# A state-space layer's recurrence: four PSUM banks for the broadcasts of delta, two for those of delta times x, and the convolution's taps over two steps

## The reference, cut to what matters

```python
u = up_x @ W_up + b_up
left, right = jnp.split(u, 2, axis=-1)
xp = jnp.pad(left, ((0, 0), (K - 1, 0), (0, 0)))
conv = sum((conv_w[:, k] * xp[:, k:k + Lq, :] for k in range(K))) + conv_b      # K = 3
x = jax.nn.silu(conv)
delta = jax.nn.softplus(x @ W_delta + b_delta)
Bm = x @ W_B + b_B
Cm = x @ W_C + b_C
dA = jnp.exp(delta[..., None] * A)
dBx = delta[..., None] * Bm[:, :, None, :] * x[..., None]
# over the tokens:  h = dA_t * h + dBx_t ;  y_t = einsum('bdn,bn->bd', h, C_t)
gated = (y + D_skip * x) * jax.nn.silu(right)
return gated @ W_down + b_down
```

## Time and profile before

| | |
|---|---|
| device time, median of 3 runs | 1930.89 us (1929.56 to 1931.49) |
| the profiled execution | 1928.22 us, of which the span of the profile is 1926.4 us |
| PE busy over the span | 1773.1 us (92%) |
| DVE busy | 1467.3 us (76%) |
| ACT busy | 902.1 us (47%) |
| POOL busy | 752.5 us (39%) |
| the loop of this layer | from 1269 to 1732 us of the span |

### The profile page before, as it was taken

The page is one execution under the profiler, slowest core; times in us unless marked ns, Lnnn a source line. Parts: engine busy times, 40 slices in busy tenths (PEclk is TensorE's granted clock), DMA queues, the critical chain, the costliest instruction groups (busy, mean ns, idle before and its releaser), DMA issues. The chain is left out here.

```text
span 1926.4 us, 23846 instructions
## 1 busy us (share of the span) xinstructions
PE 1773.1 (92%) x7613; PEld 938.9 (49%) x7613; DVE 1467.3 (76%) x2421; ACT 902.1 (47%) x2115; POOL 752.5 (39%) x850
## 2 busy tenths in 40 slices
PE   6879999999999799989998999988898988889999
PEld 2346654555555466646665555533332333335555
DVE  5868865655555488857777788789999999988886
ACT  3335544555546355435565333455465554333332
POOL 4832222334333223332210000068989899770000
PEclk9989999999999899979999999999999999899999
DMA  6000000000000000010000000000000000000000
GB/s 257 1 1 1 1 0 1 1 1 1 1 1 1 1 1 1 1 44 1 2 2 1 1 1 1 1 17 6 12 1 17 1 11 6 1 1 1 1 6 17
DMA packets 9787, 20.20 MB, mean 10 GB/s; under 512 B 1088, under 2 KB 8384, under 8 KB 8768
## 3 DMA queue, kind: packets, MB, share of 16 engines
q1 hardware_dynamic: 9664, 18.68, 2.8%
HBM read 14.48 MB, written 1.05 MB: 8 GB/s over the span
## 5 line engine op out<-in xcount | busy, mean ns | idle before, releaser
L2103 POOL TENSOR_TENSOR ssm_hc<-ssm_h,ssm_cm 128x512 f32<-128x512 f32 x256 | 324.5, 1288 | 47.3 <-DVE ssm_h L2157 46.1
L307 PE MATMUL banks<-ffn_x_high,up_high 128*128 128x512 f32 x544 | 282.2, 519 | 10.2 <-ACT ffn_s1g L857 6.2
L2042 PE MATMUL banks<-ssm_hc,const 128*128 128x512 f32 x512 | 269.1, 608 | 0.2
L2157 DVE TENSOR_TENSOR_SCAN ssm_h<-banks,ssm_dbx 128x512 f32<-128x512 f32 x208 | 248.0, 1207 | 5.3 <-issue 3.3
L2087 ACT ACTIVATE banks<-banks,a_neg 128x510 f32<-128x510 f32 x256 | 167.1, 659 | 171.4 <-PE banks L2018 170.0
L309 PE MATMUL banks<-ffn_x_high,up_low 128*128 128x512 f32 x544 | 216.1, 397 | 0.0
L308 PE MATMUL banks<-ffn_x_low,up_high 128*128 128x512 f32 x544 | 215.9, 397 | 0.0
L1504 POOL TENSOR_SCALAR wide_pin<-wide_pin,wide_rden 128x256 f32<-128x256 f32 x256 | 117.6, 478 | 223.0 <-DVE wide_rden L1522 223.0
L343 POOL TENSOR_TENSOR x_norm<-x_centred,x_square 128x512 f32<-128x512 f32 x32 | 41.5, 1297 | 392.9 <-ACT x_square L338 392.9
L1739 ACT ACTIVATE ffn_th<-banks 128x512 f32<-128x512 f32 (+1 forms) x136 | 81.2, 597 | 213.7 <-PE banks L309 191.6
L307 PEld LDWEIGHTS banks<-ffn_x_high,up_high 128*128 128x128 f32 x544 | 102.7, 189 | 98.8 <-issue 43.9
(11 more groups left out here) (228 smaller groups left out, 3518.1 us busy)
## 6 DMA issues: line engine op xcount, KB each, us to landing
ssm_packed<-ssm_parts SPq DMA_DIRECT2D x48, 64.0 KB, 2.0
up_whole<-in_up SPq DMA_DIRECT2D x1, 2304.0 KB, 14.9
weights<-in_weights SPq DMA_DIRECT2D x1, 2048.0 KB, 23.2
up_whole<-in_up SPq DMA_DIRECT2D x1, 2048.0 KB, 7.9
half<-in_half SPq DMA_DIRECT2D x1, 1440.0 KB, 17.9
weights<-in_weights SPq DMA_DIRECT2D x1, 1168.0 KB, 25.4
weights<-in_weights SPq DMA_DIRECT2D x1, 1152.0 KB, 7.9
const<-in_const SPq DMA_DIRECT2D x1, 1042.0 KB, 9.9
```

The source lines that it names most:

```text
L307: pe.matmul(out, w_high, x_high, start=True, stop=False)
L2042: pe.matmul(k.bank[5][:], k.c("hot")[:, P - row:2 * P - row], hc[:, i % LAG, :], start=False, stop=(i % NP == NP - 1)).then_inc(s["red"], 1)
L2103: pool.tensor_tensor(hc[:, i % LAG, :], h[:, i % HOLD, :], cm[:, i // NP % 2, :], ALU.mult) \
L2157: dve.tensor_tensor_scan(h[:, n % HOLD, :], k.bank[DELTA[n % AHEAD]][:], product, 0.0, ALU.mult, ALU.add).then_inc(s["h"], 1)
```

## The change

Four things are changed together.

1. `DELTA` gets a fourth bank (bank 6), and `DELTA_X` keeps two (2 and 3). PE, in turn i, now does `spread_delta(i + 1)` and then `spread_dx(i + 1)`. `spread_delta(i + 1)` waits for the scan of step i - 3, `spread_dx(i + 1)` for the product or the copy of step i - 1.
2. ACT's copy for a pooled step k is made in turn k, after the exponential of step k, where it was made in turn k - 1 before the exponential of step k - 1. The place of POOL's product among POOL's instructions stays what it was (it is written at the head of a turn where it was written at the end of the turn before).
3. The convolution: two taps at step 22, the third at step 23.
4. Every piece behind it is one step later: SiLU at 24, delta at 31, and so on to the last cut at 58.

```diff
-    AHEAD, HOLD, LAG = 3, 4, 6
-    DELTA, DELTA_X = (0, 1, 4), (2, 3, 6)
+    AHEAD, BEHIND, HOLD, LAG = 4, 2, 4, 6
+    DELTA, DELTA_X = (0, 1, 4, 6), (2, 3)
...
+    def convolve(pe, tap):
+        return pe.matmul(two(k.bank[7]), w(f"conv{tap}"), left[:, :, tap:L + tap], start=(tap == 0), stop=(tap == 2))
...
         if n == 22:
             pe.wait_ge(s["right_in"], p + 1)
             pe.wait_ge(s["cleared"], 1)
-            for tap in range(3):
-                ins = pe.matmul(two(k.bank[7]), w(f"conv{tap}"), left[:, :, tap:L + tap],
-                                start=(tap == 0), stop=(tap == 2))
-            ins.then_inc(s["conv"], 1)
-        if n == 30:
+            for tap in range(2):
+                convolve(pe, tap)
+        if n == 23:
+            convolve(pe, 2).then_inc(s["conv"], 1)
+        if n == 31:
...
-        if n == 23:
+        if n == 24:
             act.wait_ge(s["conv"], p + 1)
...
-        if n in (50, 51, 56, 57):
-            part, v = (n - 44) // 6, (n - 44) % 6
+        if n in (51, 52, 57, 58):
+            part, v = (n - 45) // 6, (n - 45) % 6
             act.wait_ge(s["rest"], 4 * p + 2 * (part - 1) + v + 1)
...
-        if n in (46, 47, 52, 53):
-            part, v = (n - 46) // 6, (n - 46) % 6
+        if n in (47, 48, 53, 54):
+            part, v = (n - 47) // 6, (n - 47) % 6
...
-                if i >= AHEAD and by_pool(i - AHEAD):
-                    pe.wait_ge(s["dx_in"], pooled[i - AHEAD + 1])
-                elif i >= AHEAD:
-                    pe.wait_ge(s["dbx"], i - AHEAD + 1 - pooled[i - AHEAD + 1])
-                pe.matmul(k.bank[DELTA_X[i % AHEAD]][:], k.h("pick")[0:96, c * P:(c + 1) * P],
+                if i >= BEHIND and by_pool(i - BEHIND):
+                    pe.wait_ge(s["dx_in"], pooled[i - BEHIND + 1])
+                elif i >= BEHIND:
+                    pe.wait_ge(s["dbx"], i - BEHIND + 1 - pooled[i - BEHIND + 1])
+                pe.matmul(k.bank[DELTA_X[i % BEHIND]][:], k.h("pick")[0:96, c * P:(c + 1) * P],
...
             pe.wait_ge(s["resets"], 1)
+            spread_delta(0)
             spread_dx(0)
             for i in range(ALL + LAG):
                 if i + 1 < ALL:
+                    spread_delta(i + 1)
                     spread_dx(i + 1)
-                if i < ALL:
-                    spread_delta(i)
...
             for i in range(ALL):
-                if i + 1 < ALL and by_pool(i + 1):
-                    m = pooled[i + 1]
-                    act.wait_ge(s["bx"], i + 2)
-                    if m >= 2:
-                        act.wait_ge(s["pdbx"], m - 1)
-                    act.activation(dxs[:, m % 2, :], k.bank[DELTA_X[(i + 1) % AHEAD]][:], ACT.Copy).then_inc(s["dx_in"], 1)
                 act.wait_ge(s["bc"], i + 1)
                 spot_i = two(k.bank[DELTA[i % AHEAD]])[:, :, 1:]
                 act.activation(spot_i, spot_i, ACT.Exp, scale=k.a_neg[:, i % NP:i % NP + 1]).then_inc(s["da"], 1)
+                if by_pool(i):
+                    m = pooled[i]
+                    act.wait_ge(s["bx"], i + 1)
+                    if m >= 2:
+                        act.wait_ge(s["pdbx"], m - 1)
+                    act.activation(dxs[:, m % 2, :], k.bank[DELTA_X[i % BEHIND]][:], ACT.Copy).then_inc(s["dx_in"], 1)
...
-    return Stage(s, home, NP, {"ffn1": (10, 14, 15, 20, 22, 23, 26, 29, 32, 35, 39, 42, 44, 48, 52, 54, NP)},
+    return Stage(s, home, NP, {"ffn1": (10, 14, 15, 20, 22, 23, 27, 30, 33, 36, 40, 43, 45, 49, 53, 55, NP)},
```

More of the change, by code:

```diff
@@ L1926, in scalar @@
                 k.table(act, "natural_log_exp_and_others")
-        if n == 31:
+        if n == 32:
             act.wait_ge(s["delta"], p + 1)
             act.activation(z[:], k.bank[7][:], ACT.Identity, bias=w("b_delta")).then_inc(s["z"], 1)
-        if n == 32:
+        if n == 33:
             act.wait_ge(s["z"], p + 1)
@@ L1934, in scalar @@
             act.activation(e[:], e[:], ACT.Exp, scale=-1.0).then_inc(s["e"], 1)
-        if n == 33:
+        if n == 34:
             act.wait_ge(s["e"], p + 1)
             act.activation(u[:], e[:], ACT.Identity, bias=1.0).then_inc(s["u"], 1)
-        if n == 34:
+        if n == 35:
             act.wait_ge(s["b"], p + 1)
             act.activation(bm[:, p % 2, :], k.bank[7][:], ACT.Identity, bias=w("b_b")).then_inc(s["b_in"], 1)
-        if n == 37:
+        if n == 38:
             k.table(act, "natural_log_exp_and_others")
@@ L1944, in scalar @@
             act.activation(cm[:, p % 2, :], k.bank[7][:], ACT.Identity, bias=w("b_c")).then_inc(s["c_in"], 1)
-        if n == 38:
+        if n == 39:
             act.wait_ge(s["u"], p + 1)
             act.activation(ln[:], u[:], ACT.Ln).then_inc(s["ln"], 1)
-        if n in (42, 43):
-            v = n - 42
+        if n in (43, 44):
+            v = n - 43
             act.wait_ge(s["ready"], 2 * p + v + 1)
@@ L1978, in vector @@
             dve.tensor_scalar(k.a_neg[:], k.a_neg[:], -1.0, None, ALU.mult).then_inc(s["a"], 1)
-        if n == 35:
+        if n == 36:
             dve.wait_ge(s["u"], p + 1)
             link(dve.scalar_tensor_tensor(fix[:], u[:], 1.0, e[:], ALU.subtract, ALU.subtract))
-        if n == 39:
+        if n == 40:
             dve.wait_ge(s["ln"], p + 1)
             link(dve.tensor_tensor(fix[:], ln[:], fix[:], ALU.subtract))
-        if n == 40:
+        if n == 41:
             dve.scalar_tensor_tensor(delta[:], z[:], 0.0, fix[:], ALU.max, ALU.add).then_inc(s["ready"], 1)
-        if n == 41:
+        if n == 42:
             dve.wait_ge(s["ready"], 2 * p + 1)
@@ L2097, in _ @@
             for i in range(ALL):
+                j = i + 3
+                if j < ALL and by_pool(j):
+                    m = pooled[j]
+                    pool.wait_ge(s["dx_in"], m + 1)
+                    pool.wait_ge(s["b_in"], j // NP + 1)
+                    if m >= 2:
+                        pool.wait_ge(s["h"], steps[m - 2] + 1)
+                    pool.tensor_tensor(pdbx[:, m % 2, :], dxs[:, m % 2, :], bm[:, j // NP % 2, :], ALU.mult) \
+                        .then_inc(s["pdbx"], 1)
                 pool.wait_ge(s["h"], i + 1)
@@ L2108, in _ @@
                     follow.slot(i % NP)
[L2109 to L2117, removed]
             follow.rest()
@@ L2142, in _ @@
                         dve.wait_ge(s["b_in"], i // NP + 1)
-                    if i >= AHEAD:
-                        dve.wait_ge(s["h"], i - AHEAD + 1)
-                    dve.tensor_tensor(dbx[:, i % AHEAD, :], k.bank[DELTA_X[i % AHEAD]][:], bm[:, i // NP % 2, :], ALU.mult) \
+                    if i >= 3:
+                        dve.wait_ge(s["h"], i - 2)
+                    dve.tensor_tensor(dbx[:, i % 3, :], k.bank[DELTA_X[i % BEHIND]][:], bm[:, i // NP % 2, :], ALU.mult) \
                         .then_inc(s["dbx"], 1)
@@ L2153, in _ @@
                     dve.wait_ge(s["da"], n + 1)
-                    product = pdbx[:, pooled[n] % 2, :] if by_pool(n) else dbx[:, n % AHEAD, :]
+                    product = pdbx[:, pooled[n] % 2, :] if by_pool(n) else dbx[:, n % 3, :]
                     if n >= HOLD:
```

6 lines of the change are left out of this document (3 added, 3 removed).

## The result

| | before | after |
|---|---|---|
| median | 1931.01 us (1928.38 to 1931.49, 6 runs) | 1939.34 us (1935.47 to 1940.86, 6 runs) |
| ratio to before, 95% interval | | 1.0045 [1.0035, 1.0055] |
| the profiled execution | 1928.22 us | 1940.52 us |

The change made the kernel 8.3 us slower. The forecast was 1936.6 us, 5.7 us slower.

What follows compares the result with a forecast made beforehand. VectorE was taken as the bound, busy 108.37 of 113.00 us a pass. Layer start 0.3, three passes 0.8 and last pass 4.6 made 5.7 us slower: 1936.6 us on the median, own range 1934.5 to 1938.5 us.

Steps and rivals of the forecast that it cites:

- The gain at the convolution: Step 25, passes preparing a next one: scan starts 1.8 us earlier, leaving 0.8 us after the losses at steps 14 and 19.
- The copy at steps 14, 19 and 59: Later copy delays GpSimd's product and the scans: 0.55 us at 14, 0.65 at 19, 1.05 at 58 and 59 together.
- Three passes: The three passes that prepare a next one: +0.8 - 1.05, a loss of 0.25 us each, 0.8 us together.
- The 0 that I put for these steps: Steps 35 to 42 of the three passes: no shift of the scans predicted, 0 us.
- The last pass: No convolution to gain from; late copy at step 9 and low-clock reduction before the logits: 4.6 us lost.
- the 0.3 of the layer's start: Start of the layer: first product waits for one more broadcast and a reset, 0.3 us (0 to 0.6).
- Hidden copies: Rival: the copy's new place costs nothing, only 1.8 us a pass gained at step 25: 1925.8 us, chance 0.15.
- The last pass absorbs its part: Rival: in the last pass only 0 to 1.8 us of 4.6 remain, 1932 to 1933.8 us; chance 0.27.
- The clock in every pass: Rival: TensorE's stand at step 60 lowers its clock every pass, adding 3 to 5 us: 1940 to 1942 us, chance 0.10.

Runs made afterwards that it cites:

- copies early: The change with ScalarE's copy for pooled step k back in turn k - 1, before the exponential of k - 1: 1929.78 us, ratio 0.9993.
- the pieces back: The change with copies early, SiLU table load before the convolution wait, and pieces from delta on at their old steps: 1932.19 us, ratio 1.0008.
- The filler: Two bf16 matmuls without a reader in each of TensorE's turns 1 to 5: 1935.98 us added to the change, 1930.95 us added to the kernel before.
- the fastest kernel: The change with copies early except step 24's in passes preparing a next one, SiLU table load before the convolution wait, and the filler: 1925.03 us, ratio 0.9968.
- the taps alone: The kernel before, banks and copies kept, with the change's split taps and every piece behind them one step later: 1931.57 us, ratio 1.0005.
- table load ahead: The change with copies early and the SiLU table load moved before ScalarE's wait for the convolution: 1927.78 us, ratio 0.9985.
- both: The change with copies early, SiLU table load before the convolution wait, pieces at their old steps, and the filler: 1929.06 us, ratio 0.9994.

## Why the prediction was right, point by point

**The gain at the convolution.** One stall instead of two, 1.71 us, with ScalarE's block as long as before: as forecast. The net gain of a pass there, the losses of steps 14 and 19 included, was 0.9 us for 0.8.

**The copy at steps 14, 19 and 59.** 0.53, 0.60 and 1.06 us for 0.55, 0.65 and 1.05. The chain was the one reckoned: the copy behind pieces that wait, then GpSimd, which has no idle time up to the next pooled step. The copies early take all but 0.2 of the first two away, so the cause is shown. Steps 58 and 59 still lose 0.4 us then of the 1.06: there the copy is the larger part. The rest is not the cut that stands a step later, since it stays 0.4 with the pieces back; the two banks of delta times x and the order of the broadcasts are left, and no run tests them alone.

**Three passes.** 0.2 us for 0.8. The third of them gained 0.4 more than the others at step 35, and that lies in the kernel before: the instruction that is L1984 in the change (two operands in SBUF, L1981 before) took 1.57 us in its third pass and 1.15 in the other two, where it took 0.66 in every pass of the change. The 0 that I put for these steps is luck: the change gained 0.5 us a pass there and lost 0.6 at L1987, which took 1.69 us for 1.11. Neither was reckoned.

**The last pass.** 5.0 us for 4.6, with two of its terms wrongly sized, one each way, so that the sum is better than its parts. Step 9 cost the 1.8 us. At step 20 I reckoned 1.2 us more of waiting, and that came (1.89 for 0.69), but the cut itself took 2.30 us for 1.08, which I had not reckoned. At step 23 I reckoned 1.6 us and 1.0 came, since the clock had risen again when the logits ran (1.09 us for 1.75). This term is not steady: it was 0.23 when the change ran again and with the filler, though the pass lost 4.9 us in both.

**What was missed.** The term that I set at nothing beyond the 0.3 of the layer's start: in the first pass TensorE waits in each of its first turns for VectorE twice, its clock is low from 1280.85 until 1287.2 (granted 0.50 from 1281 to 1287), over two float32 pairs of 1.91 us. Before, it was low from 1276 to 1279 (granted 0.50), and no scan waited for it. The filler in the change and in the kernel before shows that this is the cause of the 1.5 us, and that the loss at step 14 of this pass hung on it too.

**The rivals.** *Hidden copies*: no, the scan of step 14 waited 0.46 us for the product. The kernel with the copies early shows what it would have been: 1929.8 us, the start's loss in it. *The last pass absorbs its part*: no, 5.0 us came. *The clock in every pass*: not as told. TensorE stood 1.72 us before `spread_dx(61)` as said, and the granted clock of the second pass was 0.98, 1.00 around step 60. When the change ran again the clock did fall there in the first pass, for 0.35 us. The 0.98 is a short fall near step 43, behind a stand of 1.95 us (a float32 pair of 1.91 us at 1462.46), and no scan shows a loss there. So stands of 1.8 us and more did not always leave the clock high, as I had read from one pass of the trace before; in its third pass it fell behind one of 1.87 us. The low clock that cost time in the change came at the start of the layer, where I had not looked.

**The sum.** The layer's 6.96 us stand against 5.7: 1.5 missed in the first pass, 0.4 too little in the last, 0.6 too much in the three. That is 1.3 of the 2.7 us between 1936.6 and 1939.3. The other 1.4 lie outside the layer or in the spread of the runs, which is larger (those of before, over all comparisons, spread by 8 us). The forecast was right by the chain that it followed and the places that it named; that the total came within 2.7 us owes something to terms that cancel.

## What to carry to other kernels

A read that gives a shared buffer back belongs on its engine ahead of whatever waits longest there, and that need not be the same place in every step: all copies early were better than all late, and the one whose broadcast stands behind the convolution was better late again, once the table load behind it had been freed of its wait. Two edits that are worth nothing alone can be worth 2.3 us together. When an operation is put behind another engine's wait, follow it to the first engine that has no idle time up to its next deadline; there the delay is paid twice (steps 14 and 19). Of four edits in one change, the move of the copy lost more than the whole loss, the later pieces were a gain with the banks in place, and the banks and the split taps were never taken apart, so which of them pays is open.

## What the runs showed of the hardware

**VectorE beside GpSimd.** The cut L353 reads two operands in SBUF. In the change it started at 1651.74, with GpSimd in the first of two products (1651.00 to 1653.50), and ended at 1654.04, 0.54 us behind the second. In the fastest kernel it met the same pair so:

```profile
1641.07 1.08 DVE L353 TENSOR_TENSOR ffn_x_low<-x_norm,ffn_x_high 128x512 fp32r<-128x512 f32 x1 [1.13 <-ACT ffn_x_high L348]
...
1640.35 2.93 POOL L2123 TENSOR_TENSOR ssm_hc<-ssm_h,ssm_cm 128x512 f32<-128x512 f32 x2
```

Here the cut took 1.08 us, and GpSimd's pair 2.93 where it took 2.50 in the change. VectorE's product with B, whose one operand is in PSUM, took 0.66 to 0.70 us in every step of every kernel. The Trainium skill (SBUF — State Buffer, "SBUF: two separate sides") has it that an operation of VectorE with two inputs in SBUF and one of GpSimd lock a shared pair of ports for the whole instruction and the other waits. The rows agree, and show that VectorE can lose to two in a row. What it loses to one depends on where it meets it: L1987 of the change, second pass, started at 1457.27, 0.12 us into one of GpSimd's products (1457.15 to 1458.42), and took 1.69 us; that of the fastest kernel started 0.75 us into one and took 1.07.

**TensorE's clock** was at 1.2 GHz behind stands of 4.40 us (last pass of the change) and 2.42 us (that of the fastest kernel), and behind a row of turns with two short waits each, 0.74 and 0.19 us (first pass). It stayed high behind one of 1.72 us. Between these the length of a single stand did not decide: behind the same stand of 1.81 us for `finish` the clock stayed high in all three passes of the kernel before and fell in two of three with the taps alone, and behind stands of 1.87 us in the kernel before it stayed high in two passes and fell in the third (a float32 pair of 1.91 us for 1.02). How far the low stretch reaches varies too: of the six kernels with the copies early, three lost 1.6 us at step 23 of the last pass (copies early, table load ahead, both) and three 0.3, with nearly the same work ahead of it.
